# Recurrence of a two-layer model on one Trainium2 core: PE's work spread over the time steps, unread matmuls added, square sum moved to DVE

## The reference, cut

```
ms = jnp.mean(jnp.square(tokens), axis=-1, keepdims=True)
x = tokens * jax.lax.rsqrt(ms + EPS) * norm_w
x = x.reshape(B, T, H, D)
a_t = jnp.tanh(a)
def step(state, x_t):
    state = jnp.tanh(jnp.einsum('bhs,hst->bht', state, a_t) + jnp.einsum('bhd,hds->bhs', x_t, b))
    mixed = jnp.einsum('bhs,hsd->bhd', state, c) + skip[None] * x_t
    return (state, mixed)
...
return tokens + outs @ w_out.T + b_out
```

## Time and profile before

| | us |
|---|---|
| median of the runs (2884.64 to 2896.22) | 2887.24 |
| profiled execution, own time | 2887.34 |
| profiled execution, span of the trace | 2885.3 |
| of it attention and feed-forward | 0 to 1819 |
| of it recurrence | 1819 to 2652 |
| of it channel mix | 2652 to 2885 |
| mean granted clock | 0.825 |

### The profile page before, as it was taken

One profiled execution on the slowest core, in us unless ns is written; L12 is line 12 of the kernel. 1 busy time (PEld: TensorE's weight loads), 2 busy tenths in 40 slices (PEclk: granted clock), 3 DMA queues, 4 the chain that ended last, 5 costly groups with the idle time before them and its releaser, 6 DMA issues. The chain is left out here.

```text
span 2885.3 us, 89560 instructions
## 1 busy us (share of the span) xinstructions
PE 2670.6 (93%) x35096; PEld 1864.7 (65%) x35096; DVE 1763.2 (61%) x4998; ACT 1040.9 (36%) x2798; POOL 1039.5 (36%) x1346
## 2 busy tenths in 40 slices
PE   5899999999999999699999999899999999998897
PEld 2455555555555555466666666688888888886665
DVE  5667666666666677589999999222222222222798
ACT  1444444444444454333333333233333333332221
POOL 4334434343434344245555555222222222221222
PEclk8999999999999999999999999555555555555999
DMA  3001111111111111100000000000000000001122
GB/s 99 23 31 38 39 38 38 38 38 38 38 38 38 38 38 38 51 31 30 29 29 29 29 29 21 28 25 22 25 24 22 25 22 25 23 25 41 43 82 81
DMA packets 91569, 103.83 MB, mean 36 GB/s; under 512 B 8624, under 2 KB 78032, under 8 KB 91216
## 3 DMA queue, kind: packets, MB, share of 16 engines
q1 hardware_dynamic: 91216, 98.67, 10.7%
HBM read 48.31 MB, written 33.55 MB: 28 GB/s over the span
## 5 line engine op out<-in xcount | busy, mean ns | idle before, releaser
L1495 PEld LDWEIGHTS ps_state<-r_state,later_pairs_a 64*64 64x64 f32 x8176 | 480.0, 214 | 68.9 <-issue 51.7
L1498 PE MATMUL ps_state<-r_state,later_pairs_a 64*64 64x16 f32 x8176 | 515.0, 267 | 0.0
L1495 PE MATMUL ps_state<-r_state,later_pairs_a 64*64 64x16 f32 x8176 | 515.0, 267 | 0.0
L1498 PEld LDWEIGHTS ps_state<-r_state,later_pairs_a 64*64 64x64 f32 x8176 | 480.0, 214 | 0.0
L1426 ACT ACTIVATE r_state<-ps_state 128x64 f32<-128x64 f32 x1024 | 229.3, 224 | 567.7 <-PE ps_state L1498 564.0
L297 POOL TENSOR_SCALAR_AFFINE_SELECT probsT<-probsT 128x512 f32<-128x512 f32 x256 | 159.9, 637 | 678.6 <-ACT probsT L384 275.4
L401 DVE CUSTOM_DVE_ANT_0 ps_near<-ps_near,mask 128x512 f32<-128x512 f32 (+1 forms) x512 | 270.5, 591 | 145.7 <-PE ps_near L502 145.2
L401 DVE CUSTOM_DVE_ANT_0 ps_far<-ps_far,mask 128x384 f32<-128x384 f32 (+1 forms) x512 | 198.6, 460 | 124.0 <-PE ps_far L502 124.0
L1452 DVE TENSOR_SCALAR r_xT<-ps_state,later_recurrence_columns 128x128 f32<-128x128 f32 x128 | 39.1, 347 | 308.7 <-PE ps_state L1543 308.7
L1234 PE MATMUL ps_down<-kept_w_downT,f_hT 128*128 128x256 f32 (+1 forms) x768 | 200.7, 390 | 1.9 <-ACT f_hT L1108 1.9
L510 PE MATMUL ps_far<-Q,K 32*128 32x256 f32 (+2 forms) x1536 | 180.4, 411 | 1.9 <-ACT probsT L384 0.5
(11 more groups left out here) (208 smaller groups left out, 5655.7 us busy)
## 6 DMA issues: line engine op xcount, KB each, us to landing
k_swap<-k_sin SPq DMA_DIRECT2D x128, 128.0 KB, 2.1
xT<-in_xT_dram SPq DMA_DIRECT2D x16, 512.0 KB, 3.9
xtok<-in_x_dram SPq DMA_DIRECT2D x16, 512.0 KB, 3.9
x_rows<-x SPq DMA_DIRECT2D x16, 512.0 KB, 2.9
f_x<-x_rows SPq DMA_DIRECT2D x64, 128.0 KB, 2.0
x_rows<-f_x SPq DMA_DIRECT2D x64, 128.0 KB, 1.7
r_x<-x_rows SPq DMA_DIRECT2D x64, 128.0 KB, 2.1
x_rows<-r_x SPq DMA_DIRECT2D x64, 128.0 KB, 2.0
```

What stands on the lines that cost most here:

```text
L1495: nc.tensor.matmul(sums[half(v), j % 2, stays, c, now], A[half(v), 3 * q, c, :], state[half(v), (j - (t == 0)) % 2, stays, c, before], sta ...
L1498: out = nc.tensor.matmul(sums[half(1 - v), j % 2, changes, c, now], A[half(v), 3 * q + 1 + was, c, :], state[half(v), (j - (t == 0)) % 2, ...
```

## The change

Work of PE for one tile, by slot. Side matmuls (`recur`) stay in every slot.

| slot | before | after |
|---|---|---|
| 1 | transposes, mix 0, mix 1 | mix 0 |
| 2 | | mix 1 |
| 3 | | transposes |
| 5 | | projection 0 |
| 6 | projection 0 and 1 | |
| 7 | | projection 1 |
| 9 | | unread matmul, 128x128 |
| 11 | | feed 0 |
| 12 | feed 0 and 1 | |
| 13 | | feed 1 |
| 15 | | unread matmul, 128x128 |

`fill` issues matmuls of one half of `w_outT` by the other into parts of `room` whose content nobody reads afterwards. Nine of 256 columns stand ahead of the first transposes, one ahead of each half of the first feed, and one in the place of each half of the projection in tile 0, which has none. The square sum becomes a mean and a variance on DVE (`bn_stats`, `bn_aggr`) at the head of its step, and POOL makes mean² + variance + eps of them in three operations. The factor `DIM ** 0.5` on `norm_w` goes away with the sum.

PE at a tile's beginning, before: end of slot 1's side matmuls, transposes, both halves of the mix, slot 2.

The diff, cut to what matters:

```diff
@@ -1389,9 +1383,13 @@
                     if exists(i, 2):
                         s = j % 2
-                        pool.wait_ge(ssq_ready, i + 3)
-                        nc.gpsimd.tensor_tensor(ms[:, s:s + 1], ssq[:, s:s + 1], rms_eps[:], ALU.add).then_inc(ms_ready, 1)
-                        pool.wait_ge(ms_ready, i + 3)
+                        pool.wait_ge(x_mv_ready, i + 3)
+                        nc.gpsimd.tensor_tensor(ms[:, s:s + 1], x_mv[:, s, 0:1], x_mv[:, s, 0:1], ALU.mult).then_inc(squared, 1)
+                        pool.wait_ge(squared, i + 3)
+                        nc.gpsimd.tensor_tensor(ms[:, s:s + 1], ms[:, s:s + 1], x_mv[:, s, 1:2], ALU.add).then_inc(ms_ready, 1)
+                        pool.wait_ge(ms_ready, 2 * i + 5)
+                        nc.gpsimd.tensor_tensor(ms[:, s:s + 1], ms[:, s:s + 1], rms_eps[:], ALU.add).then_inc(ms_ready, 1)
+                        pool.wait_ge(ms_ready, 2 * i + 6)
                         nc.gpsimd.tensor_tensor(rms[:, s:s + 1], ms[:, s:s + 1], exponent[:], ALU.pow).then_inc(rms_ready, 1)
                     if exists(i, 0):
                         if later(i, 0, 2):
...
@@ -1424,19 +1422,20 @@
                                     act.wait_ge(mix_full, 2 * i - 2)
                                 now, banks = slice(t * BATCH, (t + 1) * BATCH), slice(2 * q, 2 * q + 2)
                                 nc.scalar.activation(state[:, j % 2, banks, :, now], sums[:, j % 2, banks, :, now], ACT.Tanh).then_inc(state_ready[q], 1)
-                        if t == 0 and exists(i, 2):
-                            act.wait_ge(x_loaded[(j + 2) % UNROLL], 16 * k + 16 * ((j + 2) // UNROLL + 1))
-                            if later(i, 2, 2):
-                                act.wait_ge(ssq_ready, i + 1)
-                            nc.scalar.activation(square[:, j % 2, :], x[:, (j + 2) % UNROLL, :], ACT.Square,
-                                                 accum_out=ssq[:, j % 2:j % 2 + 1]).then_inc(ssq_ready, 1)
                 pipelined(act, step, TILES, UNROLL, LEAD, LAG)
             @block.vector
             def _(dve):
                 def step(i, j, k):
                     s = (j - 1) % 2
+                    if exists(i, 2):
+                        dve.wait_ge(x_loaded[(j + 2) % UNROLL], 16 * k + 16 * ((j + 2) // UNROLL + 1))
+                        if later(i, 2, 2):
+                            dve.wait_ge(ms_ready, 2 * i + 1)
+                        nc.vector.bn_stats(x_stats[:, j % 2, :], x[:, (j + 2) % UNROLL, :])
+                        dve.drain()
+                        nc.vector.bn_aggr(x_mv[:, j % 2, :], x_stats[:, j % 2, :]).then_inc(x_mv_ready, 1)
                     if exists(i, -2):
                         dve.wait_ge(rstd_ready, i - 1)
                         if later(i, -2, 2):
...
@@ -1517,6 +1516,21 @@
                                                      start=(c == 0), stop=False, skip_group_check=True)
                     return out
+                def project(i, j, c):
+                    s = (j - 1) % 2
+                    pe.wait_ge(outs_ready, 2 * i + (c - 1))
+                    out = nc.tensor.matmul(room[:, s, OUT, :], outs[:, s, c, :], w_outT[:, c, :], start=(c == 0), stop=(c == CC - 1))
+                    if c == CC - 1:
+                        out.then_inc(out_full, 1)
+                def fill(j, bank, columns, times, start):
+                    for n in range(times):
+                        nc.tensor.matmul(room[:, (j + 1) % 2, bank, 0:columns], w_outT[:, 0, 0:P], w_outT[:, 1, 0:columns],
+                                         start=start, stop=True, skip_group_check=True)
                 def mix(j, c):
                     s = (j - 1) % 2
...
@@ -1537,30 +1551,46 @@
                                 recur(i, j, t, q)
                             at = SIDES * t + q
                             s = (j - 1) % 2
-                            if at == 1 and exists(i, 1):
+                            if at in (1, 2) and exists(i, -1):
+                                c = at - 1
+                                if c == 0:
+                                    for side in range(SIDES):
+                                        pe.wait_ge(state_ready[side], i * STEPS)
+                                mix(j, c).then_inc(mix_full, 1)
+                            if at == 3 and exists(i, 1):
+                                if i == -1:
+                                    fill(j, OUT, DIM, 9, True)
                                 pe.wait_ge(xn_ready, i + 2)
                                 for c in range(CC):
                                     out = nc.tensor.transpose(room[:, (j + 1) % 2, TURN, c * P:(c + 1) * P], xn[:, (j + 1) % 2, c * P:(c + 1) * P], ident[:])
                                 out.then_inc(x_turned, 1)
-                            if at == 1 and exists(i, -1):
-                                for side in range(SIDES):
-                                    pe.wait_ge(state_ready[side], i * STEPS)
-                                for c in range(CC):
-                                    mix(j, c).then_inc(mix_full, 1)
-                            if at == 6 and exists(i, -1):
-                                for c in range(CC):
-                                    pe.wait_ge(outs_ready, 2 * i + (c - 1))
-                                    out = nc.tensor.matmul(room[:, s, OUT, :], outs[:, s, c, :], w_outT[:, c, :], start=(c == 0), stop=(c == CC - 1))
-                                out.then_inc(out_full, 1)
-                            if at == 12 and exists(i, 1):
-                                pe.wait_ge(xT_ready, i + 2)
-                                if exists(i, -1):
-                                    pe.wait_ge(z_added, i)
-                                for c in range(CC):
-                                    out = feed(j, c)
-                                out.then_inc(inputs_in, 1)
+                            if at in (5, 7) and exists(i, 0):
+                                c = (at - 5) // 2
+                                if i == 0:
+                                    fill(j, OUT, DIM, 1, True)
+                                else:
+                                    project(i, j, c)
+                            if at in (5, 7) and i == TILES:
+                                project(i, j, (at - 5) // 2)
+                            if at == 9 and exists(i, 0):
+                                if exists(i, 1):
+                                    pe.wait_ge(xT_ready, i + 2)
+                                fill(j, TURN, P, 1, True)
+                            if at == 15 and exists(i, 0):
+                                fill(j, TURN, P, 1, False)
+                            if at in (11, 13) and exists(i, 1):
+                                c = (at - 11) // 2
+                                if i == -1:
+                                    fill(j, OUT, DIM, 1, c == 0)
+                                if c == 0:
+                                    pe.wait_ge(xT_ready, i + 2)
+                                    if exists(i, -1):
+                                        pe.wait_ge(z_added, i)
+                                out = feed(j, c)
+                                if c == CC - 1:
+                                    out.then_inc(inputs_in, 1)
                 for i in range(-LEAD, TILES + LAG):
                     step(i, i % UNROLL, i // UNROLL)
```

More of the change, by code:

```diff
@@ L1307, in recurrence @@
         x = sb("x", [P, UNROLL, DIM])
-        square = sb("square", [P, 2, DIM])
-        ssq = sb("ssq", [P, 2])
+        x_stats = sb("x_stats", [P, 2, 6])
+        x_mv = sb("x_mv", [P, 2, 2])
         ms = sb("ms", [P, 2])
@@ L1328, in _ @@
                 nc.gpsimd.memset(eps[:], LN_EPS)
-                nc.gpsimd.memset(rms_eps[:], DIM * RMS_EPS)
+                nc.gpsimd.memset(rms_eps[:], RMS_EPS)
                 nc.gpsimd.memset(exponent[:], -0.5).then_inc(set_up, 1)
@@ L1335, in _ @@
                 nc.scalar.activation(A[:], A[:], ACT.Tanh).then_inc(w_tanh, 1)
-            @block.vector
-            def _(dve):
-                dve.wait_ge(weights.loaded, 16 * weights.LOADS)
-                nc.vector.tensor_scalar(norm_w, norm_w, DIM ** 0.5, None, ALU.mult)
         x_loaded = [sem(f"x_loaded{s}") for s in range(UNROLL)]
-        ssq_ready, ms_ready, rms_ready, xn_ready = sem("ssq_ready"), sem("ms_ready"), sem("rms_ready"), sem("xn_ready")
+        x_mv_ready, squared, ms_ready, rms_ready, xn_ready = sem("x_mv_ready"), sem("squared"), sem("ms_ready"), sem("rms_ready"), sem("xn_ready")
         x_turned, xT_ready = sem("x_turned"), sem("xT_ready")
```

## The result

The changed kernel takes 3006.74 us (median of four runs, 3004.96 to 3017.41) against 2887.23 for the kernel before: a ratio of 1.0416, 95% interval 1.0383 to 1.0449. It is 4% slower, where 2551 us was forecast, and outside the range of 2500 to 2890. The profiled execution took 3007.65 us, its span is 3005.9.

The account below looks back on a forecast made before the run. PE, busy throughout the recurrence at 1.2 GHz, was taken as the bound. At full clock a tile was 6.93 + 0.7 = 7.63 us instead of 12.88; 64 tiles save 336 us, 2887.3 to 2551 us, range 2500 to 2890.

Parts of the forecast that it names:

- Does the clock stay up?: Whole recurrence: the full clock holds through nearly all of the stage, chance 0.62, giving 2551 us.
- the clock falls and does not come back: Rival, thinnest stretch from slot 15 to slot 5: +1.15 us per tile, 2940 us (2890 to 2965), chance 0.21.
- Side's pieces 0.215, loop 0.71: Recurrence at full clock: a side's pieces take 0.215 us, its loop 0.71 us; the eight steps sum to 6.93 us.
- The small pieces don't get faster: Rival, recurrence pieces: 0.43 us per side even at the full clock, 10.7 us per tile, 2747 us, chance 0.06.
- The new wait: First half projection: PE waits for DVE's outs, a 1.5 us chain from the transposes, standing 0.7 us per tile.
- Square sum: Square sum moved from ACT to DVE and POOL: costs nothing; up to 0.6 us per tile if its cover fails.
- Start: Nine unread matmuls ahead: transposes from 1824.08 to about 1826, first tanh some 1.5 us later, the tail gives it back.

Follow-up runs that it names:

- the unread work doubled: Changed kernel plus one unread 128x256 matmul ahead of the first half projection, and 256 instead of 128 columns at slots 9 and 15: 3079.3 us.
- with four: Changed kernel with four unread 128x256 matmuls per tile (before first half projection, after second half mix, slots 9 and 15): 2771.57, 2762.26, 3142.99 and 2973.81 us.
- with six: Changed kernel with six unread 128x256 matmuls per tile (one before the first half projection, two after the mix, slots 9, 14 and 15): 2801.96 us, ratio 0.9707.
- before_nine_ahead: Kernel before with only the nine unread 128x256 matmuls added ahead of the first transposes: 2885.68 us, ratio 0.9996.
- half_no_unread: Changed kernel with the recurrence in half as many matmuls (64x32, wrong weights for half the heads), without the unread matmuls at slots 9 and 15: 2744.84 us.
- Spreading alone: Changed kernel without any unread matmuls, the spreading and the square sum on DVE kept: 2921.52 us, ratio 1.0119.
- nine in each eighth: Changed kernel plus nine unread 128x256 matmuls ahead of the first half projection of every eighth tile: 2980.09 us, ratio 1.0353.
- half the pieces: Changed kernel with the recurrence in half as many matmuls, 64x32 instead of 64x16 (wrong weights for half the heads): 2562.60 us profiled, 2822 us the other run.
- unread_four_nine: Changed kernel with four unread 128x256 matmuls per tile, and nine instead of one at slot 5 in tiles 16, 32 and 48: 2911.79 us.

## Why the prediction was wrong, point by point

**Does the clock stay up? This step failed.** I put 0.62 on it from neighbours: the attention stage with small tiles at 1.00, and 1808 to 1814 with a quarter of the time standing. Both were the wrong measure. I read busy share and gaps; the runs point to how much of the array streams. With PE busy for over 95% in each, the clock held for 24 us in the changed kernel, 119 with the unread work doubled, 652 with four (each in its one profiled run), and with six through the stage, in the profiled run by its windows and in the other three by their times. The kernel before could have told: its 819 us of 99.9% busy at 0.50 are one long example of busy pieces that do not lift it, and I named it, but under "against", beside "PE stands". `before_nine_ahead` and `half_no_unread` show falls with no want of instructions.

**What the prediction did not have at all** is PE's instruction supply. It counted matmuls, not instructions. Before, at the low clock, nothing waited for them. At the full clock PE goes through a tile's instructions in 9.3 us instead of 14.9, and it then stopped for up to 1.07 us now and then. All seventeen falls in the table come behind or at the end of such a stop; with half the instructions no wait for issue was longer than 0.3 us. That the stops are a want of instructions, and that they help the fall along, is argued from this timing; no run removed them with the work and its spacing unchanged. A stop alone is not enough, as the 19 harmless ones show.

**The rival "the clock falls and does not come back"** was the right mechanism and the right place (the fall is at the first pieces of a tile), with a chance of 0.21 and too small a price: 1.15 us per tile, 2940 us (2890 to 2965), where 2.00 us were measured. Spreading alone cost 0.52. The rest is the unread matmuls, put at 0.56 and 0.12 for the change, part of it hidden, and measured at 0.74 each. Nothing hid. The rows by line and shape (busy us, mean ns) of 1850 to 2775, and last the one of before, 1850 to 2640, show why:

```profile
L1523 PE MATMUL ps_state<-later_w_outT,r_outs 128*128 128x256 f32 x252 | 153.4, 713 | 1.0
L1531 PE MATMUL ps_state<-later_w_outT 128*128 128x128 f32 x248 | 98.4, 501 | 0.0
L1554 PE MATMUL ps_state<-later_w_outT,r_outs 128*128 128x256 f32 x246 | 127.7, 674 | 0.0
```

The projection's mean went from 674 ns to 713. Two records alone stand 0.59 us apart at the low clock (they start at 2312.24 and 2312.83), four in a row 0.43. That a first weight load stands in the open in each half is my reading of it.

**Side's pieces 0.215, loop 0.71: wrong in size.** The timeline at the full clock, a half projection, both sides, an unread matmul, both sides, feed:

```profile
1840.49 0.70 PE L1523 MATMUL ps_state<-later_w_outT,r_outs 128*128 128x256 f32 x2
1841.12 0.23 PE L1494 MATMUL ps_state<-r_state,later_pairs_a 64*64 64x16 f32 x2
...
1841.37 0.21 PE L1494 MATMUL ps_state<-r_state,later_pairs_a 64*64 64x16 f32 x2
...
1841.70 0.49 PE L1531 MATMUL ps_state<-later_w_outT 128*128 128x128 f32 x2
1842.12 0.23 PE L1494 MATMUL ps_state<-r_state,later_pairs_a 64*64 64x16 f32 x2
...
1842.37 0.21 PE L1494 MATMUL ps_state<-r_state,later_pairs_a 64*64 64x16 f32 x2
...
1842.70 0.32 PE L1515 MATMUL ps_state<-r_xT,later_pairs_b 32*64 32x128 f32 x1
```

A side is 0.25 (1842.12 to 1842.37). A piece of other work costs what lies between the side's start and the next side's, less 0.25: the half projection 0.33 + 0.63 - 0.25 = 0.71 (forecast 0.55), the unread one 0.33 + 0.42 - 0.25 = 0.50 (0.33); in the same way half a feed is 0.50 (0.39), half a mix 0.46 (0.30), the transposes 0.47 (0.35). A change of kind does not get cheaper with the clock by as much as I had halved it. The tile's sum is 16 x 0.25 + 2 x (0.71 + 0.50 + 0.46 + 0.50) + 0.47 = 8.81, and the wait adds 0.44. That is 9.25, and an undisturbed tile (the second one of the kernel with nine in each eighth) took 9.29. So even with the clock up the time would have been about 2887 - 64 x 3.6 = 2657 us, an estimate, not 2551. The loop of a step without other work is 0.77 us, not 0.71 (`before_nine_ahead`, sides at 1827.06 and 1827.83).

**The small pieces don't get faster** (0.06) is refuted: 0.25 against 0.45 us per side. With it fall, at the full clock and as the prediction applied them, two rules of the Trainium skill's page "TensorE: Matmul & The Clock Gate": the section "LDWEIGHTS (loading the stationary operand)" (eight 64-column loads in a row, an estimated 0.43) and the section "Wait — 56ns, not 53.3ns?" (25 ns from start to start): a side's sixteen records, each with a load of its own in the profile, start within 0.22 us here.

**The new wait: right in place and length of the chain, too large in what it costs.** Transposes at 1837.88, first half projection at 1839.27, 1.39 us (forecast 1.5). PE stands 0.37 by its row and 0.44 more than without a wait, where 0.7 was forecast, because its own work in between takes 0.96 us and not 0.78. It needs the full clock, as said; one unread matmul fills it for nothing (with half the pieces a tile is 7.75 us with and without it).

**Square sum: right** (ratio 1.0005). **Start: right**, the nine raise the clock midway; the transposes start at 1825.16 (forecast 1826), the first tanh at 1827.94.

## What to carry to other kernels

A TensorE that is 99% busy can still sit at 1.2 GHz: before counting on the full clock, ask how much of the array streams in the thinnest stretch, and test that one stretch first, since a change that only pays at the full clock (unread matmuls, work split into halves) is a loss at the low one. At the doubled clock instructions are used up faster (a tile's in 9.3 us here instead of 14.9); small pieces in a straight-line program can then, by the timing here, outrun their supply, and a stop of under 1 us may cost the clock where the work around it is thin. Look at single runs, not the median alone: a kernel near the edge scatters by 380 us (2762 to 3143), and margin, not speed, made the version at 2802 us the better one.

## What the runs showed of the hardware

- Instructions arrive in 16 KB packets, 3.4 to 3.9 us apart in the changed kernel's stretch at the full clock. PE's stops for issue of 0.57 to 1.07 us end 2.2 to 3.0 us after a packet began; they stand only in kernels with 64x16 pieces, and only at the full clock.
- The price of a small record is the same for 16 and 32 columns: a side of eight 64x32 records takes 0.24 us at the low clock and 0.14 at the full one, a side of sixteen 64x16 records 0.45 and 0.25. Half as many records halve a side.
- Back-to-back 128x16 records with whole-array weights start 0.2 us apart at the low clock, and 2045 us of weight loads in 2129 us do not raise it.
- Why a packet is late at one time and not at another, and what exactly decides between a stop of 0.89 us without harm (`unread_four_nine`) and one of 0.57 with a fall (the changed kernel), stays open.
